# Recurrence steps issued between the products of the last routed FFN, in one program instead of three

## The chip, the cores and the metric

One core of one Trainium2 chip runs the whole kernel. The metric is the device time of one execution in microseconds; 2227.93 us is the median of three runs (2222.33 to 2228.0).

## The reference, cut to what matters

Input x is 4 batch entries x 1024 positions x 128 features, float32. Six residual blocks follow each other:

```python
x = x + 0.5 * L0_ffn(layernorm(x))     # attention across the 4 entries, then 8 experts, top 2
x = x + L0_attn(layernorm(x))          # hierarchical attention, 16 heads
x = x + 0.5 * L0_ffn(layernorm(x))     # the same routed FFN a second time
x = x + 0.5 * L1_ffn(layernorm(x))     # "a": FFN with binarised weights, 128-512-128
x = x + L1_attn(layernorm(x))          # "p", "r": recurrence, then layernorm and an FFN
x = x + 0.5 * L1_ffn(layernorm(x))     # "z": the binarised FFN again
...
def step(state, inp):                  # 1024 positions, one after the other
    xb_t, xd_t = inp
    state = jnp.tanh(state @ A.T + xb_t)      # state: 4 entries x 32
    out = state @ C.T + xd_t
    return (state, out)
```

The step is a chain: a product with A and a tanh, 1024 times, each on the result of the one before. From the second routed FFN on, everything else at a position needs that position alone and, in the recurrence, what came before it.

## The kernel before

x stays in SBUF as 8 groups of 128 positions (positions on partitions, 4 entries, 128 features). `macaron_kernel` runs four programs one after the other: the routed FFN (`causal_moe_ffn`), the attention, the routed FFN again, then `binarize` and `second_half`. Each is written by hand per engine; the order of an engine's instructions is the order of the code, and engines meet through semaphores.

The routed FFN takes a group at a time in loops with two groups a turn. Per group TensorE does 16 up products of 128x512 (L277) and 64 down products of 128x128 (L286), one expert ahead of the other, with the small attention, norms and router of the next two groups placed between experts. ScalarE does the gelu (L193), VectorE adds each expert to x (L463).

`binarize` works once on the weights: signs on ScalarE, means and products on VectorE (L564 to L585), eight turns on TensorE (L592).

`second_half` goes over the groups again. Body g (L923 to L945) issues the 128 steps of group g: the step's product (L941), which waits for the tanh of the step before, and behind each step the pieces that a table of slots (`SLOTS`) gives to that number. A piece is one 128x128 product (L833 up, L845 down), one turn (L860), one part of the input product (L869) or half a part of the mixing product (L878). The pieces serve the FFN "a" of group g + 2, the norm "p" of group g + 1, and the mixing "r" and FFN "z" of group g - 1. ScalarE does the tanh (L1006) and the gelus in 128x128 pieces (L976). `state` and `scan` hold a step's 4 columns side by side, so VectorE reorders "p" once in a group (L719).

In float32 every product is recorded as two MATMUL instructions.

Of the kernel before, what the change touches and what calls it, by code (L numbers as in the profile page):

```python
# [4 lines left out]
F32 = mybir.dt.float32  # L5
# [10 lines left out]
ONE = 1  # L16
# [529 lines left out]
def binarize(nc, S):  # L546

    with ExitStack() as ctx:
        sgn = ctx.enter_context(nc.sbuf_tensor("sgn", [128, 2, FC, 128], F32))
        alpha = ctx.enter_context(nc.sbuf_tensor("alpha", [128, FC + 1], F32))  # L550
        banks = [ctx.enter_context(nc.psum_tensor(f"bin_turn{i}", [128, 512], F32)) for i in range(2)]
        s_sign, s_bin, s_turn = (ctx.enter_context(nc.semaphore(n)) for n in ("signs", "binarised", "bin_turned"))
        w1 = S["bin1"][:, :].rearrange("p (c d) -> p c d", d=D)
        w2 = S["bin2"][:, :].rearrange("p (c h) -> p c h", h=128)
        with nc.Block() as block:
            @block.scalar
            def _(act):
                for i, w in enumerate((w1, w2)):
                    nc.scalar.activation(sgn[:, i, :, :], w, ACT.Sign).then_inc(s_sign, 1)

            @block.vector
            def _(dve):

                dve.tensor_reduce(alpha[:, 0:FC], w1, AX.X, ALU.add, apply_absolute_value=True)  # L564
                dve.tensor_reduce(alpha[:, FC:FC + 1], w2, AX.XY, ALU.add, apply_absolute_value=True)
                dve.drain()
                dve.tensor_scalar(alpha[:, 0:FC], alpha[:, 0:FC], 1.0 / D, None, ALU.mult)
                dve.tensor_scalar(alpha[:, FC:FC + 1], alpha[:, FC:FC + 1], 1.0 / (FC * 128), None, ALU.mult)
                dve.drain()
                dve.wait_ge(s_sign, 2)  # L570
                for i, w in enumerate((w1, w2)):
                    for c in range(FC):
                        a = alpha[:, c:c + 1] if i == 0 else alpha[:, FC:FC + 1]
                        dve.scalar_tensor_tensor(sgn[:, i, c, :], sgn[:, i, c, :], a, w[:, c, :],
                                                 ALU.mult, ALU.subtract)
                dve.drain()
                for i, w in enumerate((w1, w2)):
                    dve.tensor_tensor(sgn[:, i, :, :], sgn[:, i, :, :], w, ALU.add).then_inc(s_bin, 1)

                rows = S["rows"]  # L580
                dve.tensor_tensor(rows[:, 1, :], rows[:, 1, :], rows[:, 2, :], ALU.add)
                dve.tensor_scalar(rows[:, 3, :], rows[:, 3, :], 0.5, None, ALU.mult)
                for i, n in enumerate(("bin1", "bin2")):
                    dve.wait_ge(s_turn, i + 1)
                    dve.tensor_copy(S[n][:, :], banks[i][:, :])  # L585

            @block.tensor
            def _(pe):
                for i in range(2):
                    pe.wait_ge(s_bin, i + 1)  # L590
                    for c in range(FC):
                        last = nc.tensor.transpose(banks[i][:, c * 128:(c + 1) * 128], sgn[:, i, c, :],  # L592
                                                   S["ident"][:, :])
                    last.then_inc(s_turn, 1)


def second_half(nc, S, out, s_store, tag):

    x = S["x"]
    ident, rows, bias = S["ident"], S["rows"], S["chunk_bias"]
    rnnA, rnnB, rnnC, rnnD = S["rnnA"], S["rnnB"], S["rnnC"], S["rnnD"]
    minus_half = S["minus_half"]
    with ExitStack() as ctx:
# [12 lines left out]

        NORMS = ("a", "p", "r", "z")  # L620
        FFNS = ("a", "r", "z")
        stats = {k: sb(f"stats_{k}", [128, NB, 6]) for k in NORMS}
        mv = {k: sb(f"mv_{k}", [128, NB, 2]) for k in NORMS}
# [7 lines left out]
        mixed = sb("mixed", [128, NB, D])  # L631
        resid = sb("resid", [128, NB, D])
        h_pre = [sb(f"h_pre{c}", [128, 512]) for c in range(FC)]
        h_post = [sb(f"h_post{c}", [128, 512]) for c in range(FC)]
        H = {"a": h_pre, "r": h_post, "z": h_post}
        scan = [bank(f"scan{i}") for i in range(2)]
        pre_misc, post_misc = bank("pre_misc"), bank("post_misc")
        up_pre, up_post = [bank(f"up_pre{i}") for i in range(2)], [bank(f"up_post{i}") for i in range(2)]
        MISC = {"a": pre_misc, "p": pre_misc, "r": post_misc, "z": post_misc}
        UP = {"a": up_pre, "r": up_post, "z": up_post + up_pre}  # L640
# [4 lines left out]
        s_stats = {k: sem(f"stats_{k}") for k in NORMS}  # L645
        s_root = {k: sem(f"root_{k}") for k in NORMS}
# [8 lines left out]

        def grp(g):
            return x[:, g, :, :]

        with nc.Block() as block:  # L659
            @block.sync  # L660
            def _(sp):
# [1320 lines left out]
```

## Time and profile before

| | |
|---|---|
| median of three runs | 2227.93 us (2222.33 to 2228.0) |
| profiled execution, span | 2224.9 us |
| TensorE busy over the span | 1851.9 us, 83% |
| VectorE, ScalarE, GpSimd busy | 1009.9, 862.7, 193.9 us |
| granted TensorE clock, mean of the span | 0.735 |
| first and last tanh of the recurrence | 1346.2 and 2177.3 us |

The profiled execution has no device time beside its span here; the span lies 3.0 us below the median and inside the three runs. The first routed FFN ends near 367 us, the attention near 967, the second routed FFN at 1302.6, the rest at 2224.9. A matmul counts as busy from its first to its modelled last cycle, weight loads are shown apart as PEld, and the granted clock is a share of 2.4 GHz: 1.00 is 2.4 and 0.50 is 1.2.

### The profile page before, as it was taken

What the parts mean: (1) busy time and instruction counts of PE and PEld (TensorE: products, weight loads), DVE (VectorE), ACT (ScalarE), POOL (GpSimd) and SP (SyncE); (2) the same over time, 40 slices, a digit from 0 to 9 for tenths busy, and PEclk for the clock granted to TensorE, in tenths of its full rate; (3) what the DMA queues carried; (4) which work ended last, traced back from release to release, by engine and by line L of the source; (5) the groups of instructions that cost most, each with busy time, mean ns of one, the idle gap of its engine ahead of it and who ended that gap; (6) DMA issues with size and microseconds to landing.
All of it is one profiled execution on the core that took longest, in us unless ns stands there. A gap on an engine that the chain in (4) does not pass through costs nothing. (4 is left out here: it accounts for less than half of the span.)

```text
span 2224.9 us, 37410 instructions
## 1 busy us (share of the span) xinstructions
PE 1851.9 (83%) x13672; PEld 1372.4 (62%) x13672; DVE 1009.9 (45%) x3005; ACT 862.7 (39%) x2377; POOL 193.9 (9%) x314
## 2 busy tenths in 40 slices
PE   1889896848858588558898977799999999999886
PEld 1666675447556485546666765576777777766665
DVE  3666754775866778746666642111111111111102
ACT  1434442745546456424353432232323232323231
POOL 1211201001010010012121100000000000000000
PEclk8999996969879799779999985555555555555556
DMA  6000000000000000000000000000000000000000
GB/s 156 1 1 0 0 1 1 2 1 3 2 1 3 2 2 2 1 1 1 1 0 1 1 1 1 1 1 5 1 6 1 5 1 5 1 5 1 5 1 10
DMA packets 12015, 13.03 MB, mean 6 GB/s; under 512 B 1648, under 2 KB 10640, under 8 KB 11280
## 3 DMA queue, kind: packets, MB, share of 16 engines
q1 hardware_dynamic: 11840, 10.77, 1.8%
q8 instruction: 101, 1.65, 0.3%
q14 instruction: 74, 0.61, 0.1%
HBM read 8.67 MB, written 2.10 MB: 5 GB/s over the span
## 5 line engine op out<-in xcount | busy, mean ns | idle before, releaser
L1006 ACT ACTIVATE r_state<-r_scan 32x4 f32<-32x4 f32 x1024 | 166.9, 163 | 592.6 <-PE r_scan L941 589.3
L941 PEld LDWEIGHTS r_scan<-r_state,rnnA 128*32 128x32 f32 x2048 | 186.3, 141 | 253.3 <-issue 153.6
L941 PE MATMUL r_scan<-r_state,rnnA 128*32 128x4 f32 x2048 | 275.4, 205 | 52.1 <-ACT r_state L1006 52.1
L286 PEld LDWEIGHTS f_down<-moe,f_hT 128*128 128x128 f32 x2048 | 251.3, 194 | 56.9 <-issue 54.0
L277 PE MATMUL f_up<-f_x2T,moe 128*128 128x512 f32 x512 | 248.8, 610 | 11.6 <-ACT f_hT L193 11.6
L286 PE MATMUL f_down<-moe,f_hT 128*128 128x128 f32 x2048 | 254.0, 278 | 0.0
L463 DVE SCALAR_TENSOR_TENSOR x_all<-f_down,f_weight,x_all 128x128 f32 (+1 forms) x512 | 144.1, 344 | 166.6 <-PE f_down L286 163.9
L193 ACT ACTIVATE f_hT<-f_up 128x512 f32<-128x512 f32 x256 | 149.9, 598 | 139.0 <-PE f_up L277 137.6
L1618 DVE TENSOR_TENSOR att_big<-at_ring,att_big 128x512 f16<-128x512 f32 x192 | 123.9, 685 | 49.2 <-ACT att_big L1300 48.4
L277 PEld LDWEIGHTS f_up<-f_x2T,moe 128*128 128x128 f32 x512 | 90.5, 195 | 90.0 <-issue 63.5
L1300 ACT ACTIVATE att_big<-at_ring 128x512 f16<-128x512 f32 x192 | 111.4, 596 | 66.5 <-PE at_ring L1433 64.6
L761 DVE TENSOR_TENSOR x_all<-r_post_misc,x_all 128x512 f32<-128x512 f32 x8 | 5.5, 692 | 233.4 <-PE r_post_misc L845 233.4
L1433 PE MATMUL at_ring<-at_keys,att_Mhi 128*128 128x512 f16 x256 | 81.7, 403 | 30.2 <-DVE at_coarse_q L1605 18.6
L833 PE MATMUL r_up_post<-r_nT_r,mlp 128*128 128x128 f32 x256 | 94.9, 483 | 1.3 <-DVE r_nT_r L725 0.9
L845 PE MATMUL r_post_misc<-bin,r_h_post 128*128 128x128 f32 x256 | 93.1, 474 | 1.2 <-ACT r_h_post L976 1.2
L845 PE MATMUL r_post_misc<-mlp,r_h_post 128*128 128x128 f32 x256 | 93.1, 474 | 1.2 <-ACT r_h_post L976 1.2
L1725 DVE SCALAR_TENSOR_TENSOR att_big<-at_ring,att_big 128x512 f16<-128x512 f32 x128 | 80.8, 682 | 27.2 <-ACT att_big L1341 27.1
L1523 PE MATMUL at_s<-att_Nhi,att_big 128*128 128x128 f16 x1024 | 92.8, 222 | 0.0
L1341 ACT ACTIVATE att_big<-at_ring 128x512 f16<-128x512 f32 x128 | 68.7, 602 | 61.4 <-PE at_ring L1514 61.0
L1523 PE MATMUL at_s<-att_Nlo,att_big 128*128 128x128 f16 x512 | 89.3, 222 | 0.0
L1452 PEld LDWEIGHTS at_s<-at_keys,att_big 128*128 128x128 f16 x768 | 64.5, 99 | 38.4 <-issue 19.5
L1452 PE MATMUL at_s<-at_keys,att_big 128*128 128x16 f16 x768 | 72.1, 172 | 18.5 <-DVE att_big L1618 18.5
(241 smaller groups left out, 3202.2 us busy)
## 6 DMA issues: line engine op xcount, KB each, us to landing
x_all<-in_x SPq DMA_DIRECT2D x4, 512.0 KB, 6.1
moe<-in_moe SPq DMA_DIRECT2D x2, 1024.0 KB, 7.1
out<-x_all SPq DMA_DIRECT2D x8, 256.0 KB, 2.3
bin<-in_bin SPq DMA_DIRECT2D x2, 256.0 KB, 7.6
mlp<-in_mlp SPq DMA_DIRECT2D x2, 256.0 KB, 6.0
att_big<-in_att_wq SPq DMA_DIRECT2D x1, 512.0 KB, 11.2
att_big<-in_att_wk SPq DMA_DIRECT2D x1, 512.0 KB, 13.2
att_big<-in_att_wv SPq DMA_DIRECT2D x1, 512.0 KB, 14.9
```

The costliest lines, as they stand in the source:

```text
L193: nc.scalar.activation(hT[c % H_RING][:, :], up[c % UP_RING][:, :], ACT.Gelu_apprx_tanh).then_inc(s_h, 1)
L277: nc.tensor.matmul(up[c % UP_RING][:, :], w1[:, c * 128:(c + 1) * 128], x2T[b][:, :], start=True, stop=True).then_inc(s_up, 1)
L286: last = nc.tensor.matmul(down[e % 2][:, s * 128:(s + 1) * 128], hT[c % H_RING][:, s * 128:(s + 1) * 128], w2[:, c * 128:(c + 1) * 128], s ...
L463: last = dve.scalar_tensor_tensor(xg[:, s, :], down[e % 2][:, s * 128:(s + 1) * 128], weight[b][:, s, e:e + 1], xg[:, s, :], ALU.mult, ALU ...
L833: ins = nc.tensor.matmul(UP[k][c % len(UP[k])][:, s * 128:(s + 1) * 128], W1[k][:, c * 128:(c + 1) * 128], nT[k][g % 2][:, s * 128:(s + 1) ...
L845: ins = nc.tensor.matmul(MISC[k][:, s * 128:(s + 1) * 128], H[k][c][:, s * 128:(s + 1) * 128], W2[k][:, c * 128:(c + 1) * 128], start=(c = ...
L941: nc.tensor.matmul(scan[b][0:STATE, NB * t:NB * (t + 1)], rnnA[:, :], last, start=False, stop=(t == 127), skip_group_check=True).then_inc( ...
L1006: nc.scalar.activation(state[b][0:STATE, NB * t:NB * (t + 1)], scan[b][0:STATE, NB * t:NB * (t + 1)], ACT.Tanh).then_inc(s_tanh, 1)
L1300: nc.scalar.activation(XH[c % 2][:, :, h, :], ring[n % RING][:, :].rearrange("p (q i) -> p q i", i=BLK), ACT.Copy).then_inc(s_xhi, 1)
L1452: nc.tensor.matmul(o, lh, keys[:, blk, 0, :], start=True, stop=False)
L1523: last = nc.tensor.matmul(sbk[t % 2][:, 0:D], y[t % 2][:, h, :], att[w][:, h * D:(h + 1) * D], start=(h == 0 and n == 0), stop=(h == HEADS ...
L1618: dve.tensor_tensor(XL[c % 2][:, :, h, :], ring[n % RING][:, :].rearrange("p (q i) -> p q i", i=BLK), XH[c % 2][:, :, h, :], ALU.subtract) ...
```

## The change

The second routed FFN, `binarize` and `second_half` become one program, `ffn_and_recurrence`. With G = g + 1 and h = g - 1, turn g of its loop (g from -1 to 8) issues: the mixing of group h, the experts of group G (with the front work of G + 1 and G + 2 between them as before), then "r" of h, "a" of G, "z" of h, "p" and the input product of G. Behind this work `spend` counts nanoseconds that the code assigns to each instruction (245 for a 128x128 product, 470 for a 128x256 half), and issues one of the 128 steps of group g each time the sum passes `QUOTA[g]`. `pause(n)` issues up to n steps with nothing between. The first turn (g = -1) has no steps.

Up products are issued as two halves of 256 columns in two banks shared by all FFNs, gelus as halves of 256; the PSUM plan follows. States and step inputs are ordered by batch entry, so a step reads 4 columns that lie 128 apart, the reordering copy becomes a straight one, the four input products become one of 512 columns, and the mixing reads its columns side by side. ScalarE's order is worked out from the step numbers at which TensorE issued a product and needs its gelu (`issued`, `needed`). The wait of SyncE for the loads ahead of the second routed FFN goes; the group-wise stores stay.

```diff
-PHASES = ("ffn", "attn", "ffn", "second")
+PHASES = ("ffn", "attn", "last")
...
-                    for t in range(128):
-                        pe.wait_ge(s_tanh, ONE + 128 * g + t)
-                        nc.tensor.matmul(scan[b][0:STATE, NB * t:NB * (t + 1)], rnnA[:, :], last, start=False,
-                                         stop=(t == 127), skip_group_check=True).then_inc(s_step, 1)
-                        run(plan, t)
...
+                def step():
+                    n = scanned[0]
+                    g, t = divmod(n, 128)
+                    at = lambda tile, i: tile.rearrange("p (s t) -> p s t", t=128)[:, :, i]
...
+                    pe.wait_ge(s_tanh, ONE + n)
+                    nc.tensor.matmul(at(scan[b][0:STATE, :], t), rnnA[:, :], last, start=False,
+                                     stop=(t == 127), skip_group_check=True).then_inc(s_step, 1)
+                    scanned[0] += 1
...
+                def spend(ns):
+                    credit[0] += ns
+                    if credit[0] >= quota[0] and scanned[0] < limit[0]:
+                        step()
+                        credit[0] = min(credit[0] - quota[0], quota[0])
...
+                def p_input(g):
+                    pe.wait_ge(s_nT["p"], ONE + g + 1)
+                    nc.tensor.matmul(scan[g % 2][0:STATE, :], rnnB[:, :], nT["p"][g % 2][:, :], start=True,
+                                     stop=False, skip_group_check=True)
+                    spend(900)
...
+                for g in range(-1, GROUPS + 1):
+                    G, h = g + 1, g - 1
+                    limit[0] = 128 * min(max(g + 1, 0), GROUPS)
+                    credit[0] = 0.0
+                    quota[0] = QUOTA[g]
+                    if h >= 0:
+                        p_mix(h)
+                    if G < GROUPS:
+                        experts(G, h)
+                    elif h >= 0:
+                        pause(14)
+                        p_turn("r", h)
+                        pause(3)
+                    second(g, G, h)
+                    pause(128)
...
+QUOTA = {-1: 0.0, 0: 450.0, 1: 520.0, 2: 520.0, 3: 520.0, 4: 520.0, 5: 480.0, 6: 480.0, 7: 300.0, 8: 0.0}
```

TensorE in the second routed FFN before, two experts of a group (`f2_up` are the up products, `f2_down` the down products, `hT` the gelus):

```order
L277 MATMUL f2_up0<-f2_x2T1,moe1 128x512
L277 MATMUL f2_up1<-f2_x2T1,moe1 128x512
L286 MATMUL f2_down1<-moe2,f2_hT2 128x128
L286 MATMUL f2_down1<-moe2,f2_hT3 128x128
L286 MATMUL f2_down1<-moe2,f2_hT2 128x128
L286 MATMUL f2_down1<-moe2,f2_hT3 128x128
L286 MATMUL f2_down1<-moe2,f2_hT2 128x128
```

The same products in the changed program, with the steps of the recurrence (`r_scan` from `r_state` and `rnnA`) between them:

```order
L852 MATMUL r_up1<-r_x2T1,moe1 128x256
L766 MATMUL r_scan0<-r_state0,rnnA 32x4
L852 MATMUL r_up1<-r_x2T1,moe1 128x256
L766 MATMUL r_scan0<-r_state0,rnnA 32x4
L877 MATMUL r_down0<-moe2,r_hT0 128x128
L877 MATMUL r_down0<-moe2,r_hT1 128x128
L766 MATMUL r_scan0<-r_state0,rnnA 32x4
L877 MATMUL r_down0<-moe2,r_hT0 128x128
L877 MATMUL r_down0<-moe2,r_hT1 128x128
L766 MATMUL r_scan0<-r_state0,rnnA 32x4
```

Products that stood together now have a step behind every one to two of them; before, a step stood behind every single piece of `second_half`, and none between the experts.

TensorE before the first step, before the change (`xn_p` is the normed group of "p", `r_scan` from `rnnB` the input product, `r_up_pre` and `r_pre_misc` the FFN "a", here of the second group):

```order
L833 MATMUL r_up_pre0<-r_nT_a,bin1 128x128 x4
L833 MATMUL r_up_pre1<-r_nT_a,bin1 128x128 x4
L860 MATMUL r_pre_misc<-ident,r_xn_p0 128x128 x4
L869 MATMUL r_scan0<-r_nT_p0,rnnB 32x128 x4
L845 MATMUL r_pre_misc<-bin2,r_h_pre0 128x128
L845 MATMUL r_pre_misc<-bin2,r_h_pre1 128x128
```

The same place in the changed program, end of its first turn and the first steps (`r_down` and `r_h_pre` the FFN "a" of the first group, `moe1` the experts of the second):

```order
L904 MATMUL r_down0<-bin2,r_h_pre1 128x128 x4
L904 MATMUL r_down0<-bin2,r_h_pre2 128x128 x4
L904 MATMUL r_down0<-bin2,r_h_pre3 128x128 x4
L789 MATMUL r_down0<-ident,r_xn_p0 128x128 x4
L914 MATMUL r_scan0<-r_nT_p0,rnnB 32x512
L852 MATMUL r_up0<-r_x2T1,moe1 128x256
L766 MATMUL r_scan0<-r_state1,rnnA 32x4
L852 MATMUL r_up0<-r_x2T1,moe1 128x256
L766 MATMUL r_scan0<-r_state0,rnnA 32x4
```

Before, products of the second group's "a" stood on both sides of the first "p"; now the turn of "p" follows the last product of the first group's "a" at once, and the steps begin behind it with the experts of the second group.

## Rows read from the trace of the kernel before

**Rows 1.** The page: busy time of each engine, clock granted in 40 slices.

```profile
PE 1851.9 (83%) x13672; PEld 1372.4 (62%) x13672; DVE 1009.9 (45%) x3005; ACT 862.7 (39%) x2377; POOL 193.9 (9%) x314
PEclk8999996969879799779999985555555555555556
```

**Rows 2.** Windows by stage: second routed FFN's start, its groups, steady recurrence, tail.

```profile
core 0: us, PE busy (x) PEld busy (x) DVE busy (x) ACT busy (x) POOL busy (x), PEclk, DMA share, GB/s
967.00:1007.00 40.00, 15.48 (x38) 9.12 (x39) 17.89 (x70) 6.01 (x11) 11.06 (x20) 0.57 0.00 0
1007.00:1302.60 295.60, 274.36 (x1533) 197.45 (x1531) 186.36 (x769) 125.81 (x204) 50.42 (x84) 0.97 0.00 1
...
1651.70:1762.30 110.60, 109.59 (x489) 79.27 (x488) 18.86 (x62) 33.10 (x177) 5.09 (x8) 0.50 0.01 3
...
2177.30:2224.90 47.60, 28.40 (x152) 24.85 (x152) 11.77 (x34) 9.18 (x33) 2.41 (x4) 0.71 0.04 12
```

**Rows 3.** Timeline (start, length in us), recurrence steps with a piece behind each.

```profile
1700.84 0.27 PE L941 MATMUL r_scan<-r_state,rnnA 128*32 128x4 f32 x2
...
1701.04 0.80 PE L845 MATMUL r_post_misc<-mlp,r_h_post 128*128 128x128 f32 x2
1701.15 0.16 ACT L1006 ACTIVATE r_state<-r_scan 32x4 f32<-32x4 f32 x1 [0.49 <-PE r_scan L941]
...
1701.77 0.27 PE L941 MATMUL r_scan<-r_state,rnnA 128*32 128x4 f32 x2
```

**Rows 4.** Timeline, steps with nothing between, clock at 0.50.

```profile
1407.46 0.27 PE L941 MATMUL r_scan<-r_state,rnnA 128*32 128x4 f32 x2 [0.25 <-ACT r_state L1006]
...
1407.98 0.27 PE L941 MATMUL r_scan<-r_state,rnnA 128*32 128x4 f32 x2 [0.25 <-ACT r_state L1006]
```

**Rows 5.** Timeline, steps with nothing between, clock at 1.00.

```profile
1349.79 0.23 PE L941 MATMUL r_scan<-r_state,rnnA 128*32 128x4 f32 x2 [0.25 <-ACT r_state L1006]
1350.27 0.23 PE L941 MATMUL r_scan<-r_state,rnnA 128*32 128x4 f32 x2 [0.25 <-ACT r_state L1006]
```

**Rows 6.** Timeline, products back to back, clock at 1.00.

```profile
1291.82 1.95 PE L286 MATMUL f_down<-moe,f_hT 128*128 128x128 f32 x16
```

**Rows 7.** Timeline, products back to back, clock at 0.50, and a single one.

```profile
2191.68 2.56 PE L833 MATMUL r_up_post<-r_nT_r,mlp 128*128 128x128 f32 x11
...
1700.49 0.42 PE L845 MATMUL r_post_misc<-mlp,r_h_post 128*128 128x128 f32 x1
```

**Rows 8.** Windows where the clock fell or rose, columns as in rows 2.

```profile
1302.60:1307.00 4.40, 0.00 (x0) 0.00 (x0) 3.47 (x12) 1.15 (x2) 0.00 (x0) 1.00 0.00 0
1307.00:1309.20 2.20, 0.03 (x1) 0.03 (x1) 2.12 (x8) 0.00 (x0) 0.00 (x0) 0.50 0.00 0
...
1317.20:1324.00 6.80, 6.02 (x27) 5.62 (x28) 2.97 (x13) 2.28 (x8) 1.21 (x2) 0.50 0.00 1
1324.00:1330.50 6.50, 5.53 (x49) 5.32 (x49) 0.69 (x1) 2.20 (x9) 0.00 (x0) 1.00 0.00 0
...
1351.40:1370.00 18.60, 16.28 (x88) 11.13 (x86) 3.34 (x14) 6.46 (x36) 1.21 (x2) 0.50 0.00 1
```

**Rows 9.** Timeline, the chain from "a" to the input product before the first step.

```profile
1313.25 0.81 DVE L700 BATCH_NORM_STATS2 r_stats_a<-x_all 128x6 f32<-128x128 f32 x4
...
1330.53 0.69 DVE L732 SCALAR_TENSOR_TENSOR r_resid<-r_pre_misc,rows 128x512 f32<-128x512 f32 x1 [4.08 <-PE r_pre_misc L845]
...
1336.40 0.66 PE L860 MATMUL r_pre_misc<-ident,r_xn_p 128*128 128x128 f32 x4 [1.52 <-DVE r_xn_p L711]
...
1338.21 1.92 PE L869 MATMUL r_scan<-r_nT_p,rnnB 128*32 128x128 f32 x8 [1.15 <-DVE r_nT_p L719]
```

**Rows 10.** One line's instructions: the tanh, number, length in ns, first and last start.

```profile
L1006 ACT ACTIVATE r_state<-r_scan x1024: 162/163/165, 1346.2 to 2177.3; 32x4 f32<-32x4 f32 x171
```

**Rows 11.** Groups by line: one ScalarE table load (count, busy us, mean ns).

```profile
L193 ACT ACT_TABLE_LOAD x16 | 20.5, 1283 | 9.7 <-PE f_up L277 7.7 <-PE f_down L286 1.9
```

**Rows 12.** Timeline, VectorE in the second routed FFN's start.

```profile
987.10 1.15 DVE L357 TENSOR_REDUCE f_scores<-f_pairs 128x64 f32<-128x512 f32 x2 [11.16 <-POOL f_pairs L142]
```

More of the change, by code:

```diff
@@ L543, in layouts_second_half @@
     }
[L546 to L594, printed above, removed]
@@ L635, in second_half @@
         H = {"a": h_pre, "r": h_post, "z": h_post}
+        sgn = sb("sgn", [128, 2, FC, 128])
+        alpha = sb("alpha", [128, FC + 1])
         scan = [bank(f"scan{i}") for i in range(2)]
[L637 to L640, printed above, removed]
+        up = [bank(f"up{i}") for i in range(2)]
+        down = [bank(f"down{i}") for i in range(2)]
+        turn, front = bank("turn"), bank("front")
+        MISC = {"a": down[0], "p": down[0], "r": down[1], "z": down[1]}
+        TURN = {"a": down[0], "p": down[0], "r": front, "z": down[1]}
         W1 = {"a": S["bin1"], "r": S["mlp1"], "z": S["bin1"]}
@@ new lines, in v_after @@
+                def v_after(g):
+                    dve.wait_ge(s_proj, ONE + g + 1)
+                    dve.tensor_tensor(after[:, :, :], turn[:, :].rearrange("p (s d) -> p s d", d=D),
+                                      hs[g % 2][:, :, :], ALU.add)
+                    dve.drain()
+                    for s in range(NB):
+                        dve.bn_stats(stats2[:, s, :], after[:, s, :])
+                    dve.drain()
+                    for s in range(NB):
+                        last = dve.bn_aggr(mv2[:, s, :], stats2[:, s, :])
+                    last.then_inc(s_stats2, 1)
@@ new lines, in residual, with n_stats @@
+                def residual(g):
+                    xg = grp(g)
+                    dve.scalar_tensor_tensor(xg, after[:, :, :], 0.5, xg, ALU.mult, ALU.add)
+                    dve.drain()
+                def n_stats(k, g, src):
+                    dve.drain()
+                    for s in range(NB):
+                        dve.bn_stats(sstats[k][:, s, :], src[:, s, :])
+                    dve.drain()
+                    for s in range(NB):
+                        last = dve.bn_aggr(smv[k][:, s, :], sstats[k][:, s, :])
+                    last.then_inc(s_sstats[k], 1)
@@ new lines, in _ @@
+                binarise()
+                v_scores(0)
+                v_shift(0)
+                v_stats(1)
+                v_values(0)
+                v_norm1(1)
+                v_heads(0)
+                bin_out()
+                v_after(0)
+                v_norm2(0)
+                residual(0)
+                v_logits(0)
+                v_scores(1)
+                v_shift(1)
+                v_weights(0)
+                for g in range(-1, GROUPS + 1):
+                    G, h = g + 1, g - 1
+                    if h >= 0:
+                        v_mix(h)
+                    if G < GROUPS:
+                        experts(G, h)
+                    elif h >= 0:
+                        n_norm("r", h, mixed)
+                        n_T("r", h)
+                        v_resid(h)
+                    second(G, h)
```

925 lines of the change are left out of this document (662 added, 263 removed).

## Prediction

> **What bounds the kernel now.** I read the page first, then windows by stage, then the timeline of single steps. The page puts TensorE far ahead of the others, 1851.9 us against 1009.9 for VectorE and 862.7 for ScalarE, and its line of the granted clock splits the kernel in two: mostly near full speed up to the 24th slice, then sixteen slices at about half [rows 1]. The windows give the same by stage. The second routed FFN's eight groups take 295.6 us, 36.95 each, with TensorE busy 274.36 us at a granted clock of 0.97, so 2.4 GHz with short falls. A steady group of the recurrence takes 110.6 us, with TensorE busy 109.59 us at 0.50, which is 1.2 GHz [rows 2]. The reader is to see that both stages are bound by TensorE already, one at each clock: there is hardly an idle stretch in either for the other's work.
>
> The steps say why a group takes 110.6 us. With one product behind it a step takes 1701.77 - 1700.84 = 0.93 us, 0.925 over several [rows 3]. The bare round trip, step, tanh, next step, takes only 0.52 us at this clock [rows 4] and 0.48 at 2.4 GHz [rows 5]. So with a piece behind each step the tanh is back early, and TensorE, not the chain, sets the pace. Products back to back cost, at 1.2 GHz, (2.56 - 0.42) / 10 = 0.214 us per instruction, so 0.428 per product [rows 7]; at 2.4 GHz 16 instructions in 1.95 us, so at most 0.244 and, by half of 0.428, at least 0.214 per product [rows 6]; I use 0.23. A step between two products therefore adds 0.925 - 0.428 = 0.497 us to TensorE at 1.2 GHz: its own two matmuls of 4 columns and the pipeline emptying and filling around them.
>
> **The clock.** It rose in this stretch after products alone had kept TensorE busy for 6.02 of 6.80 us, and it fell after TensorE had done nothing for 4.40 us [rows 8]. From 1351.4 on it stood at 0.50 with a step behind every piece, and stayed there in steady groups with TensorE busy 99% of the time [rows 2, 8]. Being busy was not enough: steps with pieces between them never brought it up in the recurrence, products alone did.
>
> [...]
>
> **The change, part by part.** Up to 967 us nothing is touched.
>
> *Start of the merged program.* Norm, turns, projections and attention of groups 0 and 1 stay, 40.0 us [rows 2]. The binarisation moves in there. Its VectorE work lies ahead of the score reduction, where VectorE waited 11.16 us for the products on GpSimd [rows 12], so I cost it at nothing; without that wait it would cost its own time, about 6 us.
>
> *First group's experts*, without steps: 36.95 us.
>
> *First group's "a" and "p"*, with nothing beside them: before, the statistics started at 1313.25 and the input product ended at 1338.21 + 1.92 = 1340.13, 26.9 us [rows 9]. The second group's turn in there (about 1.4) goes, the last expert's addition ahead of it (about 1.3) comes in: 27 us. What matters more is the wait in it. From 1330.53 to the turn at 1336.40, 5.9 us, VectorE and GpSimd update, norm and root; before, up products of the second group filled part of it, now TensorE has nothing. An idle stretch of that kind ended at 0.50 before [rows 8], so I let the first step meet 1.2 GHz. It stands at 967 + 40 + 37 + 27 = 1071 us.
>
> *The eight groups of steps.* I count TensorE's work of a group from its order, in products of 128x128: a steady turn has 56 halves (112), 64 + 48 down products, 4 output and 4 query-key-value projections (4 + 12), mixing 8, input 4, 28 turns (half a product each, 14) and the router (4): 270. In front of 124 of the 128 steps stands some of it, 4 are bare. At 1.2 GHz: 270 x 0.428 + 124 x 0.497 + 4 x 0.52 = 115.6 + 61.6 + 2.1 = 179.3 us. Before, the same work took 36.95 + 110.6 = 147.6 us. The loss is plain: the experts' products go from 2.4 to 1.2 GHz, and since the steps already sat between pieces at TensorE's pace, nothing idle is filled. Counted the same way, turn 0 has 190 products' worth and 25 bare steps, 145.5 us; turn 1 274, 181.0; turns 2 to 4 three times 179.3; turn 5 256 and 1 bare, 173.2; turn 6 244 and 7 bare, 168.1; turn 7, where no next group is left, 76 and 73 bare, 97.8. Together 1303.5 us, against 831 us from first to last tanh [rows 10] and seven groups of experts, 259.
>
> *Tail*: mixing, "r" and "z" of the last group, as before, 47.6 us [rows 2].
>
> Edits with no cost of their own: gelus in halves (ScalarE's load of a group was 33.1 + 125.8 / 8 = 48.8 us, VectorE's 18.9 + 23.3 = 42.2 [rows 2], both far under 179); the straight copy of "p" instead of the reordering one; one input product for four; stores by SyncE, unchanged in number. The tanh now reads and writes 4 columns that lie apart. No row shows that; from nothing to the whole of a tanh again, 0.16 us [rows 3], and at 1.2 GHz the 0.4 us between bare and paced step cover either. On ScalarE's queue a tanh can now stand behind a gelu of 256 columns or a table load; who waits is the next step and all of TensorE behind it. A gelu fits in those 0.4 us, a load of 1.28 [rows 11] does not quite.
>
> *Sum*: 1071 + 1303.5 + 47.6 = 2422 us of span, against 2224.9 before. The runs' median lies 3 us over the span. I take 15 off for a spell at 2.4 GHz: between output projection and the query-key-value product seven products have a single step among them, the nearest thing to products alone. Forecast 2410 us.
>
> **Rivals.**
> 1. *The clock holds at 2.4 GHz.* The place is the stretch just named, in each of turns 1 to 4; if the clock rises there it may hold, since TensorE then is not idle for microseconds. A step between products at 2.4 GHz has no row: not under its own matmuls, 0.23 [rows 5], not over 0.497; I take the middle, 0.36. A steady turn is then 270 x 0.23 + 124 x 0.36 + 4 x 0.48 = 108.6 us. Turns 0 to 6 by the same counts, turn 7 left at 97.8 as it is mostly bare, give 834, and the kernel 1071 + 834 + 48 = 1953 us. Against it: the first step meets 1.2 GHz, and four bare steps and the wait for the mixing end each turn, where it could fall again. It decides by turns: each at 2.4 saves 70.7 us, and from (2422 - 2225) / 70.7 = 2.8 turns on the change is faster. Three to five such turns give 2070 to 2210.
> 2. *ScalarE's table loads end up on the chain.* The order has 23 in the merged program; were each 1.283 us in front of a tanh that TensorE needs at once, 29.5 us come on top: 2452 us. For it: three per turn, at the changes between gelu, exp and gelu. Against: at 1.2 GHz most of a load is covered.
> 3. *No change*: about two and a half turns at 2.4 GHz, near 2228.
>
> **How the numbers follow.** Forecast (1.2 GHz nearly throughout, 2300 to 2450) 0.61, rival 2 0.04. Of rival 1, all turns (1940 to 2040) 0.10, some turns (2040 to 2220) 0.22. No change 0.03. A measurement of this kernel tells some 0.3% from no change (the three runs lie 0.25% apart). So faster 0.32, same 0.03, slower 0.65. The range reaches from 2040 to 2460: it takes in the forecast with its bounds, the table loads and the turns in part at 2.4 GHz, and leaves out the case with all turns at 2.4. The forecast's own range is 2300 to 2450.
>
> **What would show it.** Right: a granted clock of 0.50 from about 1070 us on, first tanh near there, 128 steps taking about 179 us in turns 2 to 4, a step with two products or one half behind it 1.35 us, and VectorE and ScalarE idler than before. Wrong: a clock at 1.00 over whole turns with steps about 0.8 us apart, or ScalarE's loads as the releasers of long idle stretches on TensorE. If the first step meets 2.4 GHz, the step on the wait before the turn of "p" has failed.

## The result and the profile after

The changed kernel takes 2389.99 us (median of 4 runs, 2369.62 to 2405.72) against 2227.97 for the kernel before, a ratio of 1.071 with a 95% interval of 1.066 to 1.076: slower, and 20 us under the forecast of 2410. The profiled execution took 2389.97 us, with a span of 2388.2. Its page, busy time by engine and the clock in 40 slices, with four groups of instructions (busy us, mean ns, then the idle time ahead of them):

```profile
PE 2025.7 (85%) x13496; PEld 1427.6 (60%) x13496; DVE 1007.5 (42%) x3005; ACT 842.0 (35%) x2344; POOL 191.7 (8%) x314
PEclk8999996789697897685555766855556555555556
L1047 ACT ACTIVATE r_state<-r_scan 32x4 f32<-32x4 f32 x1024 | 170.3, 166 | 917.7 <-PE r_scan L766 916.9
L766 PE MATMUL r_scan<-r_state,rnnA 128*32 128x4 f32 x2048 | 270.0, 202 | 33.1 <-ACT r_state L1047 33.1
L877 PE MATMUL r_down<-moe,r_hT 128*128 128x128 f32 x1024 | 283.5, 423 | 0.0
L852 PE MATMUL r_up<-r_x2T,moe 128*128 128x256 f32 x512 | 274.2, 645 | 4.2 <-ACT r_hT L1119 4.2
```

Beside [rows 1], TensorE is busy 174 us longer, 2025.7 against 1851.9, while VectorE and ScalarE do no more than before. The tanh line waits 916.9 us for TensorE, and TensorE's steps wait 33.1 us for the tanh: TensorE paces the recurrence. Windows of the eight turns (from first tanh to first tanh), of the tail, and two stretches of the start; columns as in [rows 2], the clock behind PEclk:

```profile
1098.50:1248.30 149.80, 140.94 (x547) 91.25 (x547) 32.02 (x125) 41.03 (x183) 8.39 (x13) 0.50 0.00 1
1248.30:1399.20 150.90, 144.23 (x663) 97.10 (x664) 44.15 (x166) 47.01 (x200) 12.38 (x21) 0.68 0.01 2
1399.20:1547.60 148.40, 142.35 (x663) 94.80 (x663) 44.05 (x166) 47.08 (x199) 12.38 (x21) 0.68 0.01 3
1547.60:1732.40 184.80, 178.76 (x663) 118.62 (x664) 44.06 (x166) 47.01 (x200) 12.38 (x21) 0.50 0.01 2
1732.40:1904.50 172.10, 166.06 (x663) 110.33 (x664) 44.05 (x166) 47.06 (x200) 12.39 (x21) 0.56 0.01 2
1904.50:2079.90 175.40, 172.95 (x651) 115.53 (x651) 38.48 (x144) 44.10 (x192) 6.03 (x10) 0.50 0.01 2
2079.90:2248.40 168.50, 166.46 (x625) 110.14 (x626) 27.60 (x93) 41.35 (x187) 4.82 (x8) 0.50 0.01 2
2248.40:2345.10 96.70, 77.95 (x370) 51.07 (x370) 11.08 (x33) 26.97 (x144) 2.41 (x4) 0.50 0.01 3
2345.10:2388.20 43.10, 27.35 (x120) 21.82 (x120) 11.07 (x33) 6.83 (x17) 2.41 (x4) 0.70 0.02 6
...
980.20:1020.90 40.70, 19.00 (x57) 11.35 (x57) 22.57 (x76) 8.00 (x17) 10.25 (x16) 0.58 0.00 0
1020.90:1067.40 46.50, 40.83 (x229) 35.75 (x229) 25.95 (x104) 17.69 (x46) 8.24 (x15) 0.83 0.00 1
```

What is called 2.4 GHz, a granted clock of 1.00, shows in the attention of the kernel before, in f16 products of 512 columns, one instruction each:

```profile
402.79:404.51 1.72, 1.72 (x11) 0.78 (x9) 1.72 (x4) 1.44 (x4) 0.00 (x0) 1.00 0.00 0
402.79 0.59 PE L1433 MATMUL at_ring<-at_keys,att_Mhi 128*128 128x512 f16 x2
403.22 0.38 PE L1433 MATMUL at_ring<-at_keys,att_Mlo 128*128 128x512 f16 x1
403.44 0.59 PE L1433 MATMUL at_ring<-at_keys,att_Mhi 128*128 128x512 f16 x2
403.87 0.38 PE L1433 MATMUL at_ring<-at_keys,att_Mlo 128*128 128x512 f16 x1
404.08 0.59 PE L1433 MATMUL at_ring<-at_keys,att_Mhi 128*128 128x512 f16 x2
404.51 0.38 PE L1433 MATMUL at_ring<-at_keys,att_Mlo 128*128 128x512 f16 x1
```

Eight of them start in 404.51 - 402.79 = 1.72 us, 2.38 columns per ns; 1.2 GHz is half of that, by the share 0.50.

Turn 3 shows the loss: at 0.50 throughout, busy 178.76 of 184.80 us. Before, the same work took 36.95 us of experts at 0.97 and 110.6 us of recurrence at 0.50 [rows 2], 147.6 in all. Turns 1, 2 and 4 have spells in them, stretches at 1.00. Steps with two products each, first at 0.50 and then in a spell that is about to end, in TensorE's timeline (start, length):

```profile
1301.48 1.22 PE L877 MATMUL r_down<-moe,r_hT 128*128 128x128 f32 x4
1302.63 0.27 PE L766 MATMUL r_scan<-r_state,rnnA 128*32 128x4 f32 x2
1302.83 1.22 PE L877 MATMUL r_down<-moe,r_hT 128*128 128x128 f32 x4
...
1486.81 0.71 PE L877 MATMUL r_down<-moe,r_hT 128*128 128x128 f32 x4
1487.45 0.23 PE L766 MATMUL r_scan<-r_state,rnnA 128*32 128x4 f32 x2
1487.61 0.71 PE L877 MATMUL r_down<-moe,r_hT 128*128 128x128 f32 x4
1488.25 0.23 PE L766 MATMUL r_scan<-r_state,rnnA 128*32 128x4 f32 x2
1488.40 0.61 PE L837 MATMUL r_turn<-wrouter,r_x2T 128*128 128x8 f32 x4
1488.95 0.23 PE L766 MATMUL r_scan<-r_state,rnnA 128*32 128x4 f32 x2
1489.10 0.61 PE L837 MATMUL r_turn<-wrouter,r_x2T 128*128 128x8 f32 x4
```

At 0.50 a step with two products takes 1302.83 - 1301.48 = 1.35 us; at 1.00 it takes 1487.61 - 1486.81 = 0.80. In the second place TensorE works on without a gap, but on the router's products of 8 columns with steps between, and the clock falls at 1490.3. Windows around it:

```profile
1488.20:1490.20 2.00, 2.00 (x19) 1.76 (x17) 1.75 (x6) 0.33 (x2) 0.00 (x0) 1.00 0.00 0
1490.40:1500.00 9.60, 9.57 (x36) 6.11 (x35) 5.45 (x23) 2.71 (x9) 1.21 (x2) 0.50 0.01 2
```

Busy 2.00 of 2.00 us and then half the clock. Of the six spells in the eight turns two ended like this, three in the bare steps and the mixing at a turn's end, and one behind waits of 0.62 and 2.41 us. The time of a run goes with its mean granted clock (2369.62 us at 0.701, 2405.72 at 0.687), so the scatter, wider than before's, is at least in part that of the spells.

### The profile page after: what moved, and what is told of

It is laid out like the page before. It is cut to its first block, busy times and chain, and to the rows that moved or that the text cites. A ratio compares the mean times of both kernels' runs of the same rounds, so it can differ in the third digit from the quotient of the medians.

```text
span 2388.2 us, 36502 instructions
## 1 busy us (share of the span) xinstructions
PE 2025.7 (85%) x13496; PEld 1427.6 (60%) x13496; DVE 1007.5 (42%) x3005; ACT 842.0 (35%) x2344; POOL 191.7 (8%) x314
## 3 DMA queue, kind: packets, MB, share of 16 engines
q8 instruction: 105, 1.72, 0.3%
## 4 chain that ended last, share of the span: by engine, by line
issue 54%; POOL 3%; POOLq 1%; PE 0%; DVE 0%; ACT 0%; DVEq 0%; ACTq 0%
POOL r_pairs L716 1%; POOLq L685 1%; POOL r_roots L708 0%; POOL r_root_a L725 0%; POOL r_root_r L725 0%; POOLq L724 0%; POOL r_root_p L725 0%; POOL r_root_z L725 0%; PE r_up L852 0%; PE r_down L904 0%; POOLq L699 0%; POOLq L707 0%; POOLq L697 0%; POOLq L695 0%; POOLq L692 0%
## 5 line engine op out<-in xcount | busy, mean ns | idle before, releaser
L1047 ACT ACTIVATE r_state<-r_scan 32x4 f32<-32x4 f32 x1024 | 170.3, 166 | 917.7 <-PE r_scan L766 916.9
L766 PE MATMUL r_scan<-r_state,rnnA 128*32 128x4 f32 x2048 | 270.0, 202 | 33.1 <-ACT r_state L1047 33.1
L877 PE MATMUL r_down<-moe,r_hT 128*128 128x128 f32 x1024 | 283.5, 423 | 0.0
L1311 DVE SCALAR_TENSOR_TENSOR x_all<-r_down,r_weight,x_all 128x128 f32<-128x128 f32 x256 | 72.1, 344 | 492.8 <-PE r_down L877 492.8
L852 PE MATMUL r_up<-r_x2T,moe 128*128 128x256 f32 x512 | 274.2, 645 | 4.2 <-ACT r_hT L1119 4.2
L877 PEld LDWEIGHTS r_down<-moe,r_hT 128*128 128x128 f32 x1024 | 213.2, 290 | 5.3
L286 PEld LDWEIGHTS f_down<-moe,f_hT 128*128 128x128 f32 x1024 | 125.5, 194 | 27.8 <-issue 26.6
L852 PEld LDWEIGHTS r_up<-r_x2T,moe 128*128 128x128 f32 x512 | 123.5, 293 | 13.5 <-ACT r_hT L1119 5.2
L277 PE MATMUL f_up<-f_x2T,moe 128*128 128x512 f32 x256 | 123.8, 608 | 5.8 <-ACT f_hT L193 5.8
L286 PE MATMUL f_down<-moe,f_hT 128*128 128x128 f32 x1024 | 126.9, 278 | 0.0
L193 ACT ACTIVATE f_hT<-f_up 128x512 f32<-128x512 f32 x128 | 75.0, 597 | 69.4 <-PE f_up L277 68.7
L1119 ACT ACTIVATE r_hT<-r_up 128x256 f32<-128x256 f32 x256 | 92.9, 372 | 12.2 <-PE r_up L852 12.0
## 6 DMA issues: line engine op xcount, KB each, us to landing
att_big<-in_att_wv SPq DMA_DIRECT2D x1, 512.0 KB, 13.9
```

Source lines behind the costliest of these rows:

```text
L277: nc.tensor.matmul(up[c % UP_RING][:, :], w1[:, c * 128:(c + 1) * 128], x2T[b][:, :], start=True, stop=True).then_inc(s_up, 1)
L286: last = nc.tensor.matmul(down[e % 2][:, s * 128:(s + 1) * 128], hT[c % H_RING][:, s * 128:(s + 1) * 128], w2[:, c * 128:(c + 1) * 128], s ...
L766: nc.tensor.matmul(at(scan[b][0:STATE, :], t), rnnA[:, :], last, start=False, stop=(t == 127), skip_group_check=True).then_inc(s_step, 1)
L852: ins = nc.tensor.matmul(up[u % 2][:, half], weights, rhs[:, half], start=(j == 0), stop=True, skip_group_check=True)
L877: ins = nc.tensor.matmul(down[e % 2][:, s * 128:(s + 1) * 128], hT[c % H_RING][:, s * 128:(s + 1) * 128], w2[:, c * 128:(c + 1) * 128], st ...
L1047: nc.scalar.activation(at(state[b][0:STATE, :]), at(scan[b][0:STATE, :]), ACT.Tanh).then_inc(s_tanh, 1)
```

## Experiments

Theory A is the prediction's: steps between the products keep TensorE at 1.2 GHz, products without steps bring 2.4. The rivals: the clock is low for a reason that has nothing to do with the steps (B), the step is dear wherever it stands (C), and ScalarE's table loads stand on the chain. All kernels but e8 carry three small edits to the choice of tanhs that ScalarE places ahead of its other work, needed once steps stand elsewhere. Alone, they are e7:

```
-                        need("h", u - 2, 1)
+                        need("h", u - 2, 0)
+                        need("h", u - 2, 1)
-                    issued["exp", g + 2] = issued["gexp", g + 1] = scanned[0] + 1
+                    issued["exp", g + 2] = issued["gexp", g + 1] = scanned[0]
-                    tanhs(min(n, needed.get(key, n), limit[0]))
+                    tanhs(min(n, needed.get(key, issued.get(key, n)), limit[0]))
```

> The changed kernel with nothing but the three small edits to which tanhs ScalarE places ahead of its other work, which the holds needed. Every theory: as the changed kernel, 2360 to 2410 us; anything below 2300 would mean that the gain of the holds comes in part from these edits.

Measured: 2344.8 us (2323 to 2428), 1.051 of before (1.045 to 1.056). All five runs lie outside the expected range, none below 2300. The four faster ones have a mean granted clock of 0.706 to 0.716 against 0.687 to 0.701 in the changed kernel, the slowest 0.675; whether the edits or chance bring that is not shown. Beside e7, e1 to e6 below are 80 us faster and more.

### Where the steps stand

e1, all steps at the turn's end:

```
-QUOTA = {..., 0: 450.0, 1: 520.0, ..., 6: 480.0, 7: 300.0, 8: 0.0}
+QUOTA = {..., 0: 1e9, 1: 1e9, ..., 6: 1e9, 7: 300.0, 8: 0.0}
```

> All 128 steps of a turn stand bare behind the turn's products. Theory A (steps between products keep TensorE at 1.2 GHz, products alone bring 2.4): the 270 products of a steady turn run mostly at a granted clock of 1.00, 270 x 0.23 = 62 us, some 10 to 15 us of waits of the second FFN's chains come out of their cover, and the bare steps take 128 x 0.5 = 64: 136 to 142 us a turn against 148 to 185 in the changed kernel, 2130 to 2220 us in all. Theory B (the clock in the merged program is low for another reason, so where the steps stand does not matter to it): 270 x 0.428 + 64 + waits = 180 to 195 a turn, 2390 to 2480 us. Theory C (the bare step is as dear as a step between products, so only the waits change): about the changed kernel's time plus the waits, 2400 to 2480.

Measured: 2202.7 us, 0.989 of before (0.987 to 0.991), within A's range. Windows of turn 2's products and, ahead of them, turn 1's bare steps:

```profile
1373.50:1445.10 71.60, 61.98 (x404) 53.66 (x404) 40.62 (x149) 28.56 (x79) 11.06 (x19) 0.98 0.02 5
1301.80:1373.50 71.70, 41.23 (x260) 28.06 (x260) 3.08 (x17) 21.61 (x122) 1.35 (x3) 0.50 0.00 1
```

The products take 61.98 us of TensorE against the worked-out 62, at 0.98. B and C fall: the same instructions in another order are 142 us faster than e7. What is left of the turn is 9.6 us of bared waits and 71.7 us of bare steps at 0.50, 0.56 us each.

e4, the mirror image: a step behind every product, then products alone:

```
-QUOTA = {..., 0: 450.0, 1: 520.0, ..., 6: 480.0, 7: 300.0, 8: 0.0}
+QUOTA = {..., 0: 300.0, 1: 260.0, ..., 6: 260.0, 7: 300.0, 8: 0.0}
```

> A step behind every product from the turn's start (one step per 260 units), so that the 128 steps are done after some 130 products and the other 140 products of the turn stand without a step. Theory A: first half at 0.50, 128 x 0.925 = 118 us, second half at 1.00, 142 x 0.23 = 33 us and a few us of waits: 150 to 158 us a steady turn, 2230 to 2310 us; if the clock carries over into the next turn's steps and holds there, 105 a turn and about 1980. Theory B: 0.50 throughout, 180 a turn, 2380 to 2440 us.

Measured: 2264.5 us (2215 to 2268), within A's range, one run of four below it. Two windows of turn 2:

```profile
1421.40:1557.90 136.50, 135.88 (x507) 85.93 (x507) 31.49 (x115) 40.50 (x179) 9.96 (x17) 0.50 0.00 1
1557.90:1580.60 22.70, 21.42 (x145) 18.21 (x144) 12.58 (x51) 6.72 (x17) 2.41 (x4) 1.00 0.01 1
```

The turn stays at 0.50 with a step behind every product until the last step at 1554.7, rises at 1557.9 among products alone and keeps 1.00 for 99 us, 76 of them in the next turn's steps, as dense as before. The steady turns are not the expected 150 to 158 us: those with their steps at 0.50 take 161 to 164, the two with part of them at 1.00 take 114 and 115. So in this run steps held a clock that was up, for those 76 us, and in this density did not bring it up, from 1421.4 to 1554.7 us.

e2, one hold (a stretch in which no step is issued) at the turn's start:

```
+                    spent[0] += ns
+                    if spent[0] < HOLD:
+                        return
                     credit[0] += ns
-QUOTA = {-1: 0.0, 0: 450.0, 1: 520.0, 2: 520.0, 3: 520.0, 4: 520.0, 5: 480.0, 6: 480.0, ...}
+QUOTA = {-1: 0.0, 0: 405.0, 1: 465.0, 2: 465.0, 3: 465.0, 4: 465.0, 5: 440.0, 6: 420.0, ...}
+HOLD = 4400.0
```

> Each turn begins with 4400 of its 65140 units of other work (about 18 products) without a step, and the steps are packed a little tighter behind it, so that none is left bare at the end. Theory A: the clock rises in the first 10 us of every turn and then holds until something leaves TensorE with little to do, so every turn gets a spell at 1.00 of 15 to 60 us, where the changed kernel had one only by luck: 2100 to 2330 us; about 1980 if a spell lasts the whole turn (270 x 0.23 + 128 x 0.335 = 105 us). Theory B: no spell follows from it, 2370 to 2410 as the changed kernel.

Measured: 2133.8 us (2099 to 2136) beside 2226.8 for before, within A's range. Two windows of it, turn 1 and nearly all of turn 3:

```profile
1216.00:1325.90 109.90, 105.83 (x662) 72.73 (x662) 44.16 (x166) 46.90 (x200) 11.76 (x21) 1.00 0.01 3
...
1468.90:1646.40 177.50, 176.88 (x654) 117.03 (x655) 42.88 (x159) 44.65 (x194) 9.35 (x14) 0.50 0.01 2
```

A whole steady turn at 2.4 GHz takes 109.9 us where rival 1 worked out 108.6, and turn 3 at 1.2 GHz, 1468.0 to 1649.5, takes 181.5 where the forecast worked out 179.3. Turn 3 lost its spell after 3.4 us: at the hold's end TensorE waited 0.65 and 0.89 us for the gelus of the products that it had just hurried through.

e3, four holds (the edit against e2; the other quotas follow):

```
-                    if spent[0] < HOLD:
+                    if spent[0] % PERIOD < HOLD:
-QUOTA = {..., 1: 465.0, ...}
+QUOTA = {..., 1: 378.0, ...}
-HOLD = 4400.0
+HOLD = 4000.0
+PERIOD = 16285.0
```

> The same hold four times a turn (4000 units in every 16285), the steps packed to 1.5 products each between. Theory A: the clock rises in each hold, and a fall costs at most until the next one, so the mean granted clock of a steady turn is at least 0.85 and the turn takes 108 to 125 us: 1960 to 2080 us. Theory A', in which tighter steps alone pull the clock down again: spells end a few us after every hold, 2200 to 2350. Theory B: 2370 to 2420.

Measured: 2137.3 us (2134 to 2173), 0.959 of before (0.957 to 0.961), in none of the three ranges: slower than A, faster than A'. In four turns the clock fell some 30 us in, where the second hold reached the output projection early and TensorE waited 1.23 us for ScalarE's copy of the heads; it rose in the third hold and in the same four turns fell again at the router, behind a wait of 1.15 us for another such copy. Here the holds that ran into waits of 1.23 and 1.15 us lost what they had won.

### What ends a spell

e5, e2 without steps among the router's products (the quotas 1% lower, so that the steps still fit):

```
                             ins.then_inc(s_logit, 1)
-                        spend(200)
```

> As the kernel with one hold a turn, but no step stands between the router's four products of 8 columns (two to three steps a turn move elsewhere). The spells of that kernel that ended in mid turn ended there, with TensorE busy all the time. Theory A2 (what counts is how much TensorE streams, not that it is busy: steps behind products of 8 columns leave it almost nothing to stream): the spells run on past the router, and at least three of the five turns that fell at or before it stay at 1.00 to their end; 2020 to 2110 us. Rival A3 (a spell ends there by chance or by VectorE's work at the same time): no change against one hold, 2090 to 2140.

Measured: 2203.5 us (2168 to 2237), outside both ranges. No spell ended at the router any more, and one ran 314 us, through two routers: none of the four that reached it ended within 6 us of it, against three of five in e2 and two of three in the changed kernel that ended within 2.3 us. So the router went as A2 had it, the time did not; that it is the small amount TensorE streams that counts, A2's reason, is not shown by this. The hold at the start failed, as in e2's turn 3, in two turns of the profiled run, of which one is shown with the turn behind it:

```profile
1535.50:1717.80 182.30, 180.39 (x662) 118.96 (x662) 44.06 (x166) 47.04 (x199) 12.81 (x24) 0.50 0.01 2
1717.80:1827.80 110.00, 105.71 (x662) 72.60 (x662) 42.74 (x158) 46.90 (x199) 10.64 (x17) 1.00 0.01 3
```

Turns 3 and 4 do the same work, 72.3 us apart by the clock alone.

e6, holds where the products have their inputs:

```
                     for e in range(EXPERTS):
                         if e + 1 < EXPERTS:
                             e_up(g, e + 1)
+                            quiet[0] = e == 4
...
+                        quiet[0] = e in (0, 6, 7)
                         e_down(g, e)
...
+                        quiet[0] = e in (0, 3, 6, 7)
                         if e == 3 and back:
                             p_proj(g + 1)
...
+                    quiet[0] = False
                 def spend(ns):
+                    if quiet[0]:
+                        return
                     credit[0] += ns
-QUOTA = {..., 0: 450.0, 1: 520.0, 2: 520.0, 3: 520.0, 4: 520.0, 5: 480.0, 6: 480.0, ...}
+QUOTA = {..., 0: 275.0, 1: 372.0, 2: 372.0, 3: 372.0, 4: 372.0, 5: 355.0, 6: 346.0, ...}
```

> Three holds a turn, at places where the products have their inputs ready: the first expert's down products, the output projection with the query-key-value products, and the seventh and eighth experts' down products with the router between them. Theory A: no turn stays low for more than about 30 us, and the router no longer ends a spell: mean granted clock at least 0.9 in turns 1 to 6, 108 to 118 us each, 1950 to 2030 us. If the waits of the second FFN's chains end the spells (steps packed tighter there): 2040 to 2120.

Measured: 2026.1 us (2011 to 2030), 0.908 of before (0.904 to 0.912), as theory A had it, with 0.91 to 0.94 in turns 1 to 6. It is the fastest version here, and faster than the kernel before by 9% and than the changed one by 15%. Three of its turns:

```profile
1217.70:1334.00 116.30, 113.24 (x663) 78.64 (x664) 44.08 (x166) 46.94 (x199) 12.42 (x21) 0.91 0.00 1
1334.00:1447.30 113.30, 110.24 (x664) 76.64 (x664) 43.96 (x166) 47.01 (x200) 12.42 (x21) 0.94 0.01 4
1447.30:1560.50 113.20, 110.14 (x663) 76.30 (x663) 43.98 (x166) 46.94 (x200) 12.41 (x21) 0.94 0.01 3
```

Each turn from 2 to 6 still loses the clock in or right behind the mixing at its start, until the first hold 14 to 17 us later. e9 and e11 tried to close that, with no step in the mixing and behind the input product; e11 also gave up the hold at the projection and ran the last hold on through one chunk of up products; e10 is e6 with that last edit alone (the quotas follow, so that few steps or none are left bare):

```
e9, e11, in p_mix and p_input:
+                    quiet[0] = True
                     for s in range(NB):
...
                         spend(245)
+                    quiet[0] = False
-                    spend(900)
e10, e11, in p_up:
                     for c in range(FC):
+                        quiet[0] = k == "r" and c == 0
```

> The three holds, and in addition no step between the eight products of the mixing at a turn's start nor behind the input product; the steps in the rest of the turn are packed to about 1.4 products each. With the three holds every turn's spell ended in the mixing and 14 to 20 us went by at 1.2 GHz until the next hold. Theory A2 (steps between products that stream little end a spell): most turns now begin at 1.00, 106 to 110 us each instead of 113 to 116: 1975 to 2005 us. Rival (the products of 32 rows end the spell by themselves, or the tighter steps end it elsewhere): 2010 to 2050, as with three holds or slower.

> Mixing and input product held, the hold at the first expert's down products, the one around the router running on through the first chunk of the second FFN's up products, and the hold at the output projection given up, so that the steps elsewhere stand as far apart as with three holds. Theory A2: neither the mixing nor the table load ends a spell any more, 105 to 110 us a turn: 1965 to 2005 us. Rival (products of 32 rows end the spell by themselves): a fall at each turn's end, 113 to 118 a turn, 2010 to 2050.

> The kernel with three holds, the third one running on through the first chunk of the second FFN's up products, so that ScalarE's load of the gelu table finds no step in front of which TensorE has to wait. In the kernel with the mixing held, both turns that fell in mid turn fell there, with TensorE waiting 0.76 and 0.68 us around that load. Theory A2: in the kernel with three holds this place ended no spell, so there is little to win: 1995 to 2035 us, about as with three holds, and smaller scatter. Rival (the steps that are packed tighter end spells elsewhere): 2035 to 2100.

Measured: e9 2083.6 us (2046 to 2092), e11 2211.1 and e10 2209.8, 0.993 of before for both. All three missed. In e9 one of four spells outlasted the mixing by more than 3 us, though no step stood in it: the rival, that those products end a spell by themselves, is not ruled out. Two of the six spells that reached the second FFN's first up products ended there. e6 waits there as in e9, 0.76 and 0.68 us, and keeps the clock; the steps stand tighter in e9, but that this ended the two is not shown. In e10 and e11 the longer hold ended every spell there. Timeline of e10, ScalarE and TensorE:

```profile
1280.42 0.42 ACT L1093 ACTIVATE r_probs<-r_shifted 128x256 f32<-128x256 f32 x1 [3.87 <-DVE r_shifted L1225]
1281.09 1.28 ACT L1143 ACT_TABLE_LOAD   x1
1282.39 0.47 ACT L1143 ACTIVATE r_h_post<-r_up,chunk_bias 128x256 f32<-128x256 f32 x1
1283.31 0.70 PE L856 MATMUL r_up<-r_nT_r,mlp 128*128 128x256 f32 x2 [1.93 <-ACT r_h_post L1143]
```

The rest of that turn, and the same place in e6:

```profile
1284.70:1355.80 71.10, 70.24 (x272) 46.15 (x271) 13.76 (x55) 17.49 (x81) 2.41 (x4) 0.50 0.02 4
```

```profile
1287.83 0.23 PE L767 MATMUL r_scan<-r_state,rnnA 128*32 128x4 f32 x2 [0.76 <-ACT r_state L1055]
```

The exponential waits 3.87 us for VectorE, the load follows, and TensorE, early because it was held free of steps, waits 1.93 us for the first gelu. Then the clock falls, and the 71 us to the turn's end run at 0.50; so it went in all six turns from 1 to 6, after waits of 1.7 to 1.9 us.

### The table loads

e8, the changed kernel without them and e12, the same edit on e10:

```
-  probs, gate: ACT.Exp
+  probs, gate: ACT.Tanh
-  hT: ACT.Gelu_apprx_tanh
+  hT: ACT.Gelu
```

> The changed kernel with tanh in place of both exponentials and one kind of gelu in both FFNs, so that ScalarE keeps one function table in the merged program; softmax and router weights are therefore not the reference's. Theory A: each of the 23 loads was mostly covered at 1.2 GHz, so 5 to 20 us less by themselves (TensorE waited 14.0 us in all at the line behind the table load of the second FFN's gelus), and some more if a spell at 2.4 GHz is no longer cut off: 2300 to 2385. The rival that the loads stand on the chain: at least 29 us less by themselves in kernels with as many spells, and the loss against before is largely theirs: below 2300.

> The kernel whose third hold runs on through the first chunk of up products, which lost its spell in every turn where TensorE waited 1.9 us for the second FFN's first gelu, with tanh in place of both exponentials and one kind of gelu, so that ScalarE loads no table there; softmax and router weights are therefore not the reference's. The wait is made of ScalarE's wait for VectorE's shifted scores, the exponentials and the load of 1.28 us. Theory A3 (the load is what ends the spells there): the wait shrinks to some 0.65 us, the spells run on to the turn's end, 105 to 116 us a turn: 1970 to 2040 us. Rival (the place falls with the rest of that wait, or with the steps after it): 2150 to 2205, 1.3 us a turn less than with the loads.

Measured: e8 2354.8 us (2352 to 2376), e12 2045.9 us (2045 to 2047; 0.919 of before, 0.917 to 0.921). With tanh for the exponentials and one kind of gelu ScalarE indeed loads no table between them. Its table loads from 960 us on in the changed kernel, 8 + 8 + 6 + 1 = 23, and the only one in e8, at 1025.61 us ahead of the first gelu:

```profile
L1119 ACT ACT_TABLE_LOAD x8 | 10.3, 1283 | 0.1
L1134 ACT ACT_TABLE_LOAD x8 | 10.3, 1283 | 9.0 <-PE r_up L852 8.9
L1084 ACT ACT_TABLE_LOAD x6 | 7.7, 1283 | 0.1
L1090 ACT ACT_TABLE_LOAD x1 | 1.3, 1283 | 0.0
```

```profile
L1119 ACT ACT_TABLE_LOAD x1 | 1.3, 1283 | 0.0
```

At 1.2 GHz the loads matter little. Turn 5 has the same work in both and stands at 0.50 throughout, with three loads (3.85 us) in the changed kernel and none in e8; the two windows:

```profile
1904.45:2079.92 175.47, 173.02 (x651) 115.61 (x651) 38.48 (x144) 44.15 (x192) 6.03 (x10) 0.50 0.01 2
```

```profile
1891.46:2066.22 174.76, 173.03 (x651) 115.55 (x652) 38.47 (x144) 40.40 (x190) 6.04 (x10) 0.50 0.01 2
```

Without the loads it is 0.71 us shorter. As a whole e8 lies 35 us under the changed kernel, within A's range. TensorE's waits for the second FFN's gelus fall from 14.0 to 8.0 us, and the profiled run has 10 us more of spells; how much of the 35 is the loads by themselves is not separated. In e10 they decide: it has 20 of them from the first step on, 25.7 us in all, and without them it is 164 us faster. The wait of 1.93 us is now 0.61:

```profile
1291.43 0.70 PE L856 MATMUL r_up<-r_nT_r,mlp 128*128 128x256 f32 x2 [0.61 <-ACT r_h_post L1143]
```

Five of the six spells that reach this place run on; in turn 2 one still ended there, and e12 lies 6 us above A3's range. Nor does every load at 2.4 GHz cost a spell: e6 has the same 20, its TensorE, with steps between those up products, waits 0.76 and 0.68 us and keeps the clock, and it is 20 us faster than e12.

## Why the prediction was right, and where it was off

**What bounds.** Right: TensorE at both clocks, ScalarE and VectorE idler, no chain of tanhs.

**The clock at the first step.** Right, and for the reason given: 1.00 up to 1090.9 us, nothing on TensorE from 1087.8 to 1093.3 while the "p" norm runs, 0.50 behind it.

```profile
1093.30 1.12 PE L789 MATMUL r_down<-ident,r_xn_p 128*128 128x128 f32 x4 [5.55 <-DVE r_xn_p L1334]
```

**The turns.** Right in size. Worked out 145.5, 181.0, three times 179.3, 173.2, 168.1, 97.8; measured 149.8, 150.9, 148.4, 184.8, 172.1, 175.4, 168.5, 96.7. Where the clock stayed at 0.50 (turns 0, 3, 5, 6, 7) the sum is 11.3 us too low in 763.9; the step of 1.35 us came out as worked out. A lone instruction of 128 columns lasts 0.42 us at 0.50 where one more in a row adds 0.214 [rows 7]; that the 0.497 of a step is its own 0.27 [rows 3] and such a start and end around it was an estimate and fits in size. A tanh on columns that lie apart takes 166 ns instead of 163 [rows 10]. Of the gelus of 256 columns those of the experts (0.37 us) fit in the 0.4 us between bare and paced step, those of the other two FFNs (0.46) do not quite.

**The spells.** Right in kind, too small: 15 us taken off, 68.2 measured (30.1, 30.9 and 7.2 in turns 1, 2 and 4 against the working). The place was too narrow. Of six rises one came where it was expected, behind output projection and query-key-value product. Two came one expert later, behind another query-key-value product with no step between it and the down product ahead of it; the others behind three down products in a row, behind up products with which TensorE caught up after a wait of 2.41 us, and behind the input product of 512 columns.

**The start.** The step that failed: 1071 us for the first step, 1098.5 measured. VectorE's timeline of the stage's start, after and then before:

```profile
973.47 0.27 DVE L1452 MEMSET r_scores<- 128x256 f32 x1 [3.97 <-PEq L666]
...
994.78 1.67 DVE L1208 TENSOR_REDUCE r_scores<-r_pairs 128x64 f32<-128x512 f32 x4 [7.11 <-POOL r_pairs L716]
...
1002.74 1.11 DVE L1196 TENSOR_SCALAR r_xn<-x_all,r_mv,r_roots 128x128 f32<-128x128 f32 x4 [2.39 <-POOL r_roots L701]
```

```profile
967.98 0.27 DVE L504 MEMSET f_scores<- 128x256 f32 x1 [0.93 <-PEq L1916]
```

TensorE's first query-key-value product and turn of the heads, after and then before:

```profile
982.44 1.65 PE L809 MATMUL r_front<-wqkv,r_ln1T 128*128 128x384 f32 x2 [1.11 <-ACT r_ln1T L1071]
...
1008.41 1.11 PE L789 MATMUL r_turn<-ident,r_pvs 128*128 128x128 f32 x4 [15.87 <-DVE r_pvs L1244]
```

```profile
977.98 5.17 PE L245 MATMUL f_qkvb<-wqkv,f_ln1T 128*128 128x384 f32 x8 [0.87 <-ACT f_ln1T L160]
...
996.26 1.09 PE L231 MATMUL f_turn<-ident,f_pvs 128*128 128x128 f32 x4 [13.10 <-issue]
```

The 27.5 us are 13.9 up to the first up product (1020.9, not 1007), 9.5 in the first group's experts, 3.8 in "a" and "p", and 0.3. The stage began 5.5 us later, 3.0 of them a longer wait after the attention. From the first turn to the first up product it took 40.7 us against 33.2 before. The four query-key-value products, before in one run of 5.2 us, now take 8.4, as three of them wait about 0.6 us for ScalarE's copy of the one ahead. The binarisation was as free as said, 982.2 to 987.7 on VectorE ahead of a wait that is still 7.11 us ([rows 12]: 11.16); but VectorE now takes the second group's norm ahead of the first group's heads, and TensorE's turn of the heads comes 13.6 us after the score reduction instead of 9.2. The first group's experts took 46.5 us at 0.83, not 36.95 at 0.97: a mean of eight groups was used for the first, which took 41.6 before too (1009.2 to 1050.8) and now starts at 0.50. "a" and "p" took 30.8, not 27. These are readings of the trace; no run tested them.

**The tail.** 43.1 us, not 47.6. So 2422 + 27.5 + 11.3 - 68.2 - 4.5 = 2388.1 us, the span: the forecast's 2410 was close partly by luck, because the late start and the longer spells offset each other.

**Rival 1** did not come about in the changed kernel, but its prices hold: a step between products at 2.4 GHz costs 0.80 - 2 x 0.23 = 0.34 us (0.36 taken), a turn saves 182.3 - 110.0 = 72.3 (70.7). Its condition was that TensorE "is not idle for microseconds", and the router shows that this is not enough: a spell ends with TensorE busy all the time too. The bare steps and the mixing at a turn's end, named against it, did end three of the six spells. Nor did busy time by itself bring the clock up: in turn 3 TensorE was busy 178.76 of 184.80 us at 0.50.

**Rival 2** was right to be small here and wrong in kind: at 1.2 GHz the loads are mostly covered (0.71 us of 3.85 in turn 5), and in e10, at 2.4 GHz, they cost through the clock far more than through their length (164 us against e12, for 25.7 us of loads).

## What to carry over

Before interleaving a latency-bound chain with dense work, read which clock each has and what the chain's instructions do to it: the same products cost 0.23 or 0.43 us, and in turn 3 of the changed kernel a small step behind every second one kept them at 0.43. If the two must share an engine, give that engine stretches of dense work at places where the inputs lie ready and space the small steps between them, as e6 does in 2026.1 us; a stretch that ends in a wait for another engine can lose the clock it has won, as in e3 (1.23 us) and e10 (1.93 us). Judge a wait at 2.4 GHz by what follows if the clock falls, 71 us at half clock in e10, not by its length.

## What was not expected of the hardware

TensorE fell to half its clock with no gap in its work, at four products of 8 columns with steps between (busy 2.00 of 2.00 us); without those steps, in e5, no spell ended there. In e10 a wait of 1.93 us was followed by 71 us at half clock, and removing 25.7 us of table loads gave 164 us. In e4 steps behind every product did not raise the clock in 133 us of one turn and kept it at 1.00 for 76 us of the next, where it was up.
